# Winograd feed-forward: two of four operand sums formed in the first product, row factors split piece by piece, first weight factor prepared during attention

## What is computed

```python
emb = silu(_sin_emb(timestep)) @ W_ada + b_ada
x = _ln(src) * (1.0 + scale) + shift
probs = softmax(where(mask, -inf, q @ k.T / sqrt(32) + attention_bias))
x = x + ((probs @ v) @ Wo + bo)
h = _ln(x) * g2 + beta2
ff = _gelu2(h @ W1 + b1) @ W2 + b2        # _gelu2(x) = x * sigmoid(1.702 x)
return x + ff
```

## Time and profile before

| | us |
|---|---|
| median of 3 runs (2605.85 to 2611.53) | 2606.36 |
| the profiled execution's own time | 2609.52 |
| its span | 2607.7 |
| PE busy | 2414.0 (93%) |
| DVE busy | 1953.8 (75%) |
| POOL busy | 1514.2 (58%) |
| ACT busy | 1325.0 (51%) |

### The profile page before, as it was taken

One profiled execution on the slowest core, in us unless ns is written; L12 is line 12 of the kernel. 1 busy time (PEld: TensorE's weight loads), 2 busy tenths in 40 slices (PEclk: granted clock), 3 DMA queues, 4 the chain that ended last, 5 costly groups with the idle time before them and its releaser, 6 DMA issues.

```text
span 2607.7 us, 60788 instructions
## 1 busy us (share of the span) xinstructions
PE 2414.0 (93%) x21010; PEld 2232.6 (86%) x21010; DVE 1953.8 (75%) x3303; ACT 1325.0 (51%) x3663; POOL 1514.2 (58%) x1403
## 2 busy tenths in 40 slices
PE   4999999999999999878999999999979999999998
PEld 3888888888888888767898888888979999999998
DVE  4788787887878787665555555555579999999998
ACT  2666666666666666644444444444543333333332
POOL 3777777777777777674343434443554555545464
PEclk8999999999999999988999999999989999999999
DMA  7444444444444444232223222232354444454443
GB/s 228 123 131 131 132 132 132 132 131 132 131 132 131 128 130 116 63 114 106 106 105 121 105 105 112 105 121 106 130 172 132 153 153 152 146 156 150 145 153 113
DMA packets 252114, 338.69 MB, mean 130 GB/s; under 512 B 24448, under 2 KB 165888, under 8 KB 251904
## 3 DMA queue, kind: packets, MB, share of 16 engines
q1 hardware_dynamic: 251904, 336.00, 39.7%
HBM read 235.03 MB, written 100.93 MB: 129 GB/s over the span
## 4 chain that ended last, share of the span: by engine, by line
PE 19%; DVE 13%; issue 12%; POOL 6%; ACT 4%; DVEq 1%; DMA 0%; SPq 0%; POOLq 0%; ACTq 0%
PE up L1402 5%; DVE gs L1364 5%; PE up L1404 5%; PE up L1403 5%; POOL hTf L161 3%; POOL gu L1110 2%; PE turn L1402 2%; PE turn L1403 1%; PE turn L1404 1%; DVE gbuf L1355 1%; POOL gu L1109 1%; DVE gu L1355 1%; DVE r L212 1%; ACT T L244 1%; ACT p5c L1178 1%
## 5 line engine op out<-in xcount | busy, mean ns | idle before, releaser
L1402 PE MATMUL up<-T,wc 128*128 128x256 f32 x1792 | 527.9, 295 | 68.8 <-DVE gu L1274 27.2
L1404 PE MATMUL up<-T,wc 128*128 128x256 f32 x1792 | 510.1, 285 | 0.0
L1403 PE MATMUL up<-T,wc 128*128 128x256 f32 x1792 | 509.2, 284 | 0.0
L1402 PEld LDWEIGHTS up<-T,wc 128*128 128x128 f32 x1792 | 343.1, 191 | 100.0 <-ACT p1c L1173 39.7
L618 POOL TENSOR_TENSOR s<-s,rinv 128x512 f32<-128x512 f32 x256 | 266.6, 1042 | 274.4 <-DVE rinv L745 274.1
L672 ACT ACTIVATE s<-s,nmx 128x128 f32<-128x128 f32 x1024 | 396.5, 392 | 33.0 <-DVE nmx L739 27.3
L1402 PE MATMUL up<-wc,gs 128*128 128x256 f32 x1280 | 360.8, 282 | 0.0
L1403 PE MATMUL up<-wc,gs 128*128 128x256 f32 x1280 | 359.2, 281 | 0.0
L1404 PE MATMUL up<-wc,gs 128*128 128x256 f32 x1280 | 359.1, 281 | 0.0
L1403 PEld LDWEIGHTS up<-T,wc 128*128 128x128 f32 x1792 | 342.8, 191 | 0.0
L611 POOL TENSOR_TENSOR bias<-bias,mneg 128x512 f32<-128x512 f32 x256 | 335.8, 1334 | 10.7 <-DVE mneg L750 10.7
(11 more groups left out here) (188 smaller groups left out, 7109.3 us busy)
## 6 DMA issues: line engine op xcount, KB each, us to landing
bias<-in_bias SPq DMA_DIRECT2D x128, 512.0 KB, 5.4
gated<-gu SPq DMA_DIRECT2D x128, 512.0 KB, 2.6
adab<-ada_rows SPq DMA_DIRECT2D x64, 512.0 KB, 5.3
gbuf<-gated SPq DMA_DIRECT2D x64, 512.0 KB, 3.6
gu<-gated SPq DMA_DIRECT2D x64, 512.0 KB, 3.9
xin<-in_x SPq DMA_DIRECT2D x32, 512.0 KB, 4.8
resid<-rout SPq DMA_DIRECT2D x64, 256.0 KB, 2.0
r<-resid SPq DMA_DIRECT2D x16, 1024.0 KB, 5.9
```

Of the source, the lines that this page charges most:

```text
L1402: pe.matmul(out_ap, sh, mh, start=start, stop=False)
L1403: pe.matmul(out_ap, sh, ml, start=False, stop=False)
L1404: return pe.matmul(out_ap, sl, mh, start=False, stop=stop)
```

## The change

- **Gated columns.** A new POOL step `gather(k, s)` in the first product, two units late, forms slot 4 (quarter 0 + quarter 3) in a small new tile `s1p` and slot 6 (quarter 1 - quarter 0) over quarter 0 in `gu`; both are stored, so a unit of `gated` has 5 x 256 columns in place of 4 x 256, in two DMAs each way. In the second product DVE forms slots 5 and 7 alone (two operations for three) and POOL forms none (`third` is gone).
- **Row factors.** The two POOL sums of a half stand in each of two units (2 and 3, 5 and 6) in place of four in one (1 and 4); highs, lows, normalise and statistics are spread likewise, at most one piece per unit and engine; the transposes stand at units 0 and 2 in place of 0 and 3.
- **End of attention.** In the last two batches DVE takes each maximum right behind its scores and adds the residual last; after them it inverts before it adds the residual. Group 0's row factors and weight unit 0 are made ready here, the sums of weight units 1 and 2 too; weight units 1 to 5 and group 1's rows are loaded here, into tiles that the attention no longer uses.
- **Start of the feed-forward.** Only weight unit 1 is split before the first unit; sums stand three units ahead in place of two; product 3 has a bank of its own that the attention frees last.
- **Seam of the products.** W2's units are prepared at j = 1, 2, 4, 5, 7 of the last group, the last three inside the second product's group 0; gated units 0 and 1 are loaded, summed and (unit 0) split before the first product ends.

```diff
@@ POOL, feed_block
+            def gather(k, s):
+                at_least(pool, g1_done, k + 1)
+                at_least(pool, g2_done, k + 1)
+                at_least(pool, g_out[(s - 2) % 4], ((k - s) // 4 + (1 if s >= 2 else 0)) * 2 * DMA)
+                pool.tensor_tensor(s1p[:, s % 2, :], gu[:, s, 0, :], gu[:, s, 3, :], ALU.add).then_inc(g_first, 1)
+                at_least(pool, g_first, k + 1)
+                pool.tensor_tensor(gu[:, s, 0, :], gu[:, s, 1, :], gu[:, s, 0, :], ALU.subtract).then_inc(g_sums, 1)
...
-                    c22_u4(n * J + (j - 1), (j - 1) % 4)
-                if first and j + 2 < J:
-                    weights.sums(pool, j + 2)
-                if fixed(n) and n == LAST and j:
-                    weights.sums(pool, J + j - 1)
+                    c22_u4(k - 1, (j - 1) % 4)
+                if not (first and j < 2):
+                    gather(k - 2, (j - 2) % 4)
+                if first and j + 3 < J:
+                    weights.sums(pool, j + 3)
+                if fixed(n) and n == LAST and second_weights(j) is not None:
+                    weights.sums(pool, J + second_weights(j))
@@ where the pieces stand
-            return (2, 4) if first else (0, 3)
+            return (2, 4) if first else (0, 2)
...
-            return (4, 7) if first else (1, 4)
+            return ((4, 4), (7, 7)) if first else ((2, 3), (5, 6))
...
-            return ((5, 5), (7, 7)) if first else ((2, 2), (5, 5))
-
-        def lows_at(first):
-            return (6, 7) if first else (3, 6)
+            return ((5, 5), (6, 7)) if first else ((2, 3), (5, 6))
+
+        def second_weights(j):
+            return {1: 0, 2: 1, 4: 2, 5: 3, 7: 4}.get(j)
@@ SP, feed_block
-                sp.dma_start(gbuf[s][:, 0:4, :].rearrange("p q n -> p (q n)").unsqueeze(1), gated_units[:, bass.ds(k, 1), :]).then_inc(g_in[s], DMA)
+                sp.dma_start(t[:, 6, :].unsqueeze(1), gated_units[:, bass.ds(k, 1), 0:H]).then_inc(g_in[s], DMA)
+                sp.dma_start(t[:, 1:5, :].rearrange("p q n -> p (q n)").unsqueeze(1), gated_units[:, bass.ds(k, 1), H:]).then_inc(g_in[s], DMA)
@@ DVE, feed_block
+                if fixed(n) and n == LAST:
+                    if second_weights(j) is not None:
+                        for piece in range(2):
+                            weights.low(dve, J + second_weights(j), piece)
+                    if j == 7:
+                        low(0, 0)
...
-                for m, (to, a, op, b) in enumerate(A_TYPE[:2] + A_TYPE[3:]):
+                dve.tensor_tensor(t[:, 5, :], t[:, 4, :], t[:, 1, :], ALU.subtract).then_inc(s_part, 1)
+                at_least(dve, s_part, k + 1)
+                dve.tensor_tensor(t[:, 7, :], t[:, 2, :], t[:, 5, :], ALU.subtract).then_inc(s_sums, 1)
@@ SP, attention_block
-                if on.ahead == 3:
-                    sp.wait_ge(v_done, B)
+                if on.end == -7:
                     weights.load(sp, 0)
+                if on.end == -2:
+                    sp.wait_ge(second.xt_done, 4)
+                    weights.load(sp, 1)
+                    sp.wait_ge(q_done, PAIRS * G)
+                    second.load(sp, 1)
+                if on.end == 0:
+                    for m in (2, 3):
+                        sp.wait_ge(second.t_ready, 2 * (m - 1))
+                        weights.load(sp, m)
+                if on.end == 1:
+                    for m in (4, 5):
+                        weights.load(sp, m)
@@ DVE, attention_block
+                elif on.last:
                     invert(t - 1, 1 - b, G - 1)
+                    add_residual(t - 2, p - 1, (u - 1) % UNROLL, b)
```

More of the change, by code:

```diff
@@ L486, in _ @@
             low(dve, 2, range(CH // 2))
-Half = namedtuple("Half", "attn prev done mask bias proj turn gains stats load norm tail last split_o first_o ahead")
+Half = namedtuple("Half", "attn prev done mask bias proj turn gains stats load norm tail last split_o first_o end")
 def half(p, b, pairs):
@@ L626, in step @@
                     normalize_p(t - 1, 1 - b, G - 1)
+                if on.end == -1:
+                    weights.sums(pool, 1)
+                if on.end == 0:
+                    weights.sums(pool, 2)
                 if on.mask:
@@ L685, in step @@
                     copy_pT(t - 1, 1)
+                if on.end in (-3, -2):
+                    second.copy(act, 0, on.end + 3, 1)
                 if on.attn:
@@ L792, in step @@
                     norm.spread(dve, p + 3)
+                if on.end == -1:
+                    second.low(dve, 0, 0, 0, 0)
                 if on.prev:
@@ L806, in step @@
                     second.spread(dve, 0)
-                if on.ahead == 2:
-                    for m in range(second.NB):
-                        second.normalize(dve, 0, m)
-                if on.tail and b == 1:
-                    for piece in range(2):
-                        second.low(dve, 0, 0, 0, piece)
-                if on.last:
+                if on.end in (-6, -5):
+                    for m in range(2):
+                        second.normalize(dve, 0, (on.end + 6) * 2 + m)
+                if on.end == -1:
+                    second.low(dve, 0, 0, 0, 1)
+                if on.end == 0:
                     for piece in range(2):
                         second.low(dve, 0, 0, 1, piece)
+                        weights.low(dve, 0, piece)
                 if on.split_o:
@@ L1092, in down @@
                         store_y(n - 1, 1 - u, 1)
-            for j in range(1, 4):
-                weights.load(sp, j)
-            sp.wait_ge(weights.w_ready, 2)
-            norm.load(sp, 1)
             run(sp, up, down, before_down)
@@ L1248, in down @@
                     high(n * J + (j + 2), (j + 2) % 4)
-            for piece in range(2):
-                weights.high(act, 0, piece)
+                if first and j < 6:
+                    weights.high(act, J + 5 + j // 2, j % 2)
             for piece in range(2):
@@ L1342, in before_down @@
                 c12(K - 1, 3)
-                sums(0, 0)
-                low(0, 0)
-                for piece in range(2):
-                    weights.low(dve, 2 * J - 1, piece)
-                sums(1, 1)
                 low(1, 1)
@@ L1386, in down @@
                     low(n * J + (j + 2), (j + 2) % 4)
-            for m in range(2):
-                for piece in range(2):
-                    weights.low(dve, m, piece)
+                if first and j < 6:
+                    weights.low(dve, J + 5 + j // 2, j % 2)
+            for piece in range(2):
+                weights.low(dve, 1, piece)
             run(dve, up, down, before_down)
```

407 lines of the change are left out of this document (227 added, 180 removed).

## The result

| | us | ratio to before |
|---|---|---|
| before, median of 4 runs | 2608.95 (2605.85 to 2612.40) | 1 |
| changed, median of 4 runs | 2524.76 (2522.33 to 2526.22) | 0.9676 [0.9658, 0.9694] |
| forecast | 2473 (2448 to 2508) | |
| changed, the profiled execution | 2526.22, its span 2524.4 | |

The account below looks back on a forecast made before the run. PE was taken to wait on misplaced POOL work in the first product and on a DVE short of time in the second. Savings 65.6 + 27.6 + 13.2 + 10.8 + 1.4 + 9.9 + 5.5 = 134 us gave 2473 us, range 2448 to 2508.

Parts of the forecast that it names:

- What bounds the kernel now: First product loses 5.4 us a group as POOL waits for ACT's copy; second loses because DVE is busy 611.36 of 627.8.
- Second product, 27.6 us forecast: Groups 1 to 15: DVE loses 8 of 24 sums a group, both PE waits go, 41.85 to 40.0 us a group.
- My sign, one single long wait for `gs`: Sign of being right: PE waits for the split gated columns only once at length, at the seam.
- rival 3: Second product keeps its waits, from late 640 KB loads or unbroken `finish` beside DVE's first units: +27.6, 2501 us; 8%.
- Steady groups, 65.6 forecast: First product, groups 2 to 14: sums moved behind ACT's copy, no wait left, 47.5 to 42.5 us a group.
- Group 0, 13.2 forecast: First product's first group: POOL's 56 operations take 52 us, so 53 instead of 66.2 us; bounds 48 and 63.
- Last group, 1.4 forecast: First product's last group: POOL has 16 operations more for `gather`, 8 fewer for W2; 42.5 instead of 43.9 us.
- End of the attention, 5.5 forecast: Reordered residuals, the last inversion, DVE splits, SP loads and barrier: sum 5.8 us saved, taken as 5.5; bounds 0 and 10.
- 3 us each: End of attention, two batches: the residual leaves the place between scores and first maximum, saving 6 us in all.
- Group 1 and seam: First product's group 1: 44 us, 10.8 saved; seam with second product's group 0: 49.4 us, 7 of waiting kept, 9.9 saved.
- The second, full blocking of POOL and DVE: First product: `gather` waits out DVE's splits, 23 us more in steady groups and 9 in group 0: 2505 us; 22%.
- The fifth, POOL as the bound: First product: POOL's 41 operations a group set the pace and the kernel gets slower, up to 2682 us; 2%.

Follow-up runs that it names:

- the three edits: Changed kernel with closing sums paced by PE's units, weight unit 7's load ahead of unit 2's store, weight units 4 and 5's loads behind the barrier: 2475.66 us, 0.9493.
- the paced sums: Changed kernel; in second-product groups but the first, POOL waits before unit j's closing sums until PE has finished unit j-1: 2486.5 us, 0.9528.
- the kernel with all five: The three edits plus W2's sums ahead of the gather in the last group and weight unit 0's split behind the last residual: 2482.4 us, 0.9505.
- the two load edits: Changed kernel, each alone: weight unit 7's load ahead of unit 2's store, 2526.11 us; weight units 4 and 5's loads behind the barrier, 2526.74 us.

## Why the prediction was wrong

**What bounds the kernel now.** Half right. For the first product the chain from POOL's wait to PE's stall is there, but a second one, DVE's for the rows, lay under it. For the second product it was wrong: "DVE is busy 611.36 of 627.8 us. It works no backlog off" took busy time for work. Without POOL's closing sums the same DVE work took 504 us. The rows to see it were there: three sums in 3.28 or in 1.76 us.

**Second product, 27.6 us forecast (15 x 1.85 is 27.8), 5.8 lost.** This is the step that failed: DVE's time behind the drain. I charged "a split 4.0, two sums (2.2) and the next split's first piece (1.7): done at 8.6, needed at 9.9". The 2.2 came from dividing 3.28 by three. Measured behind the drain: the drain ended 2.3 us into PE's unit (which began at 2430.08), not 0.7; the split took 3.1, two sums 2.9, the first piece about 2: 10.3. A sum beside POOL is mostly a wait for POOL's operation, so in these rows taking one of three away saved 0.4 us, not 1.1. And I stopped at the first unit: the next one has the same 2.9 of sums again, and there stands the wait of 1.72 us. DVE's busy time did fall as forecast, to 34.3 us a group (34 said), and PE's waits grew all the same, because they are made in the first 15 us behind the drain and not by the sum over a group. My sign, one single long wait for `gs`, failed with 31 waits. This is the second branch of rival 3 ("all of POOL's `finish` ... beside DVE's first units"), a case put at 8% with both its branches. What spoke against it, a microsecond of room in each of six later units, was of no use, since PE waits at units 2 and 3.

**Steady groups, 65.6 forecast.** Right, with 0.45 us a group too much: 42.05 for 42.5. `gather` took 0.74 and 0.94 us an operation where 0.74 to 0.85 was said, and POOL's 32.3 us are the 32 forecast. But the reason was half of it: I credited the place of the sums, which alone gives 1.1 us a group, and had the earlier load of the rows in no step at all.

**Group 0, 13.2 forecast, nothing came.** I counted POOL's operations and no load. SP's load of weight unit 7 stands behind a store, that store behind POOL's gather, and POOL's next work is that load's sums: 4.9 of the 13.4 us in that pair of profiles. I took the group as POOL's 52 us and 1 more, and did not add up what PE itself loses. Its row has, beyond a steady group's 42.05 us, five waits of 13.3 us in all: the one of 7.28 behind that load, and four of 1.1 to 1.9 for ACT's copies. And 82 of its 336 matmuls start 0.21 us apart instead of 0.12, which is 7.6 us. Some 3.5 us stay open. The slow matmuls stand mostly behind PE's pauses, the first 27 of them behind the 9 us at the barrier, at half the full clock:

```profile
1128.18:1134.30 6.12, 6.12 (x29) 6.12 (x30) 5.30 (x7) 2.63 (x5) 4.48 (x5) 0.50 0.26 74
```

With the load ahead of the store there are 54 slow matmuls (5.0 us).

**Last group, 1.4 forecast, 3.0 lost.** I sized POOL's work and not ACT's wait for it, by the timeline above; no run mended it, so this reading is not shown by a run.

**End of the attention, 5.5 forecast, -0.4 came** in the pair of profiles, just past the lower bound of 0. One pair says little here: PE's first matmul came at 1127.7 to 1130.2 in six profiles of kernels with the attention of before (mean 1129.0) and at 1124.5 to 1129.1 in eight with the changed one (1127.3). So the change is worth some 1.7 us, still well short of 5.5. SP's eight loads held the barrier for 2.4, against 1.9. DVE's splits ahead of the last residual were put at 1.6: DVE began that residual 0.3 to 2.4 us after PE's last product with them, 0.04 in the two kernels that split behind it. The "3 us each" of the reordered batches was the large part. The distance between the starts of the scores of the last two batches fell from 13.05 to 11.74 us, while the stretch behind it, to the projection of the last batch but one, became 1.7 longer (12.42 to 14.12). PE's clock has a part in the spread: the twelve matmuls of that projection start over 4.1 to 4.8 us in five of the eight profiles (4.77 in the changed kernel's own, at a granted clock of 0.50), and there PE began at 1127.8 or later; in the other three they start over 2.65, and PE began at 1127.0 or earlier, though the next projection was slow there (4.2).

**Group 1 and seam**: within 1 us; one wait of 5.9 for the 7 said.

**The rivals.** The second, full blocking of POOL and DVE, was priced for the first product, where no wait of PE in the steady groups shows it. The Trainium skill (SBUF — State Buffer, "SBUF: two separate sides") says that such a pair exclude each other for the whole instruction; the trace agrees in the second product, where a sum of 0.42 us took 1.52 beside closing sums of 1.3 to 2.2. I had the rule in hand and applied it in the wrong stage. The fifth, POOL as the bound, was rightly small, but the point from which it decides is nearer than the sum of operations says: eight operations more cost, sixteen lose everything.

## What to carry to other kernels

An engine's busy share can hold another engine's time: compare the same operation beside a busy and beside an idle neighbour, and price what is left by the neighbour's operation, not by dividing the slow figure. Look at the stretch in which the wait is made, too: DVE's busy time a group fell as forecast and PE's wait grew. When a wait goes, look for the one that lies under it in the same unit; moving the sums alone gave 1.1 us a group and the load alone none, together 4.5. In a queue, ask where late work can stand without cost: one wait ahead of POOL's closing sums, with no work removed, took 35 us from the second product (633.6 to 598.1).

## What the runs showed that I had not expected

PE's undisturbed unit of 42 matmuls has three lengths in the second product, 4.93, 4.98 or 5.04 us, all at a granted clock of 1.00, and keeps the one it has for as long as it doesn't wait. In the unbroken runs one length lasted through the whole second product: 4.93 us in 124 of 127 distances with the three edits (groups 1 to 15 in 591.4 us), 4.98 in 121 with the paced sums (598.1), 5.04 in 122 in the kernel with all five (604.8). Where PE waits twice a group it changes at such waits. Over the second product it is worth up to 13 us, and no edit touches what PE does there. It would account for the spread of the runs of one kernel (2482.46 to 2495.68 for the paced one) and for the gains of 2 to 5 us by the two load edits, plain in their stretches, not being seen in the times; that is not shown, since each kernel has the trace of one execution only. What sets it stays open. In the first product the undisturbed distance was 5.04 us, in the kernel before and in the changed one.
